# Matrix products that nobody reads, put into three pauses of TensorE in a two-layer attention and mixture-of-experts kernel

## What is computed

```python
x = x + _L0_attn_ref(_layernorm(x, axis=-1), L0_attn_Wq, L0_attn_Wk, L0_attn_Wv, L0_attn_Wo)   # causal, 16 heads of 8
x = x + _L0_ffn_ref(_layernorm(x, axis=-1), L0_ffn_router_w, L0_ffn_router_b, L0_ffn_w1, ...)  # 2 of 8 experts, 128 -> 512 -> 128
x = x + _L1_attn_ref(_layernorm(x, axis=-1), L1_attn_wq, L1_attn_wk, L1_attn_wv, L1_attn_wo)   # linear attention, no softmax
x = x + _L1_ffn_ref(_layernorm(x, axis=-1), L1_ffn_w_gate, L1_ffn_b_gate, L1_ffn_W1, ...)      # 1 of 8 experts
```

## Time and profile before

| | us |
|---|---|
| median of 3 runs | 666.56 (665.36 to 669.21) |
| profiled execution, its own time | 669.52 |
| span of its instructions | 667.4 |
| PE busy in the span | 532.7 (80%) |
| DVE busy | 449.2 (67%) |
| ACT busy | 354.0 (53%) |
| POOL busy | 342.5 (51%) |
| mean granted clock of PE | 0.893 |

### The profile page before, as it was taken

How to read it: one execution, slowest core, us unless ns; L and a number is a source line. 1 busy time by engine, 2 the same in 40 slices (tenths; PEclk the granted TensorE clock), 3 DMA queues, 4 the chain that set the end, 5 groups by cost and what they waited for, 6 DMA issues and landing times. The chain is left out here.

```text
span 667.4 us, 15359 instructions
## 1 busy us (share of the span) xinstructions
PE 532.7 (80%) x4916; PEld 439.3 (66%) x4931; DVE 449.2 (67%) x1287; ACT 354.0 (53%) x894; POOL 342.5 (51%) x459
## 2 busy tenths in 40 slices
PE   3189999999899998865989999999167561499996
PEld 2146666666666665643889989999155450498995
DVE  6476777878998797673777755553379877365662
ACT  2014457555655565443557656665347674265653
POOL 2003334434376536665746777776441547054555
PEclk9557999999999999987899999999567885699999
DMA  6563444445455445144423332221590125323330
GB/s 167 104 147 63 101 110 110 103 102 102 97 121 123 107 94 121 39 163 170 94 57 82 97 93 81 80 75 48 154 364 20 66 71 164 84 82 88 92 101 19
DMA packets 59525, 69.37 MB, mean 104 GB/s; under 512 B 9241, under 2 KB 50657, under 8 KB 57148
## 3 DMA queue, kind: packets, MB, share of 16 engines
q1 hardware_dynamic: 51168, 52.48, 31.6%
q0 software_dynamic: 7168, 14.77, 6.8%
q10 hardware_dynamic: 1116, 1.22, 0.9%
HBM read 45.31 MB, written 23.67 MB: 103 GB/s over the span
## 5 line engine op out<-in xcount | busy, mean ns | idle before, releaser
L616 DVE TENSOR_REDUCE mx<-max_ps 128x2 f32<-128x512 f32 (+1 forms) x192 | 128.4, 688 | 53.3 <-PE max_ps L277 51.4
L457 ACT ACTIVATE pT<-sc_ps 128x1536 f32<-128x1536 f32 x64 | 92.8, 1451 | 79.0 <-PE sc_ps L305 75.4
L1189 POOL DMA_INDIRECT expert_rows<-yt,go x72 | 78.7, 1093 | 28.6 <-issue 19.8
L1367 ACT ACTIVATE hT<-h_ps,wb 128x128 f32<-128x128 f32 x288 | 78.3, 386 | 20.2 <-PE h_ps L1414 20.2
L862 POOL TENSOR_TENSOR turn<-eps 128x1 f32<-128x1 f32 x64 | 12.6, 198 | 145.4 <-ACT pT L457 145.3
L58 POOL DMA_INDIRECT expert_queues<-rxr,rseats x64 | 65.7, 1026 | 26.8 <-issue 17.4
L1255 DVE COPY wb<-wpack 128x1156 f32 x72 | 53.6, 787 | 34.3 <-issue 26.9
L1414 PE MATMUL h_ps<-xT,wb 128*128 128x128 f32 x576 | 72.0, 279 | 0.5 <-ACT xT L1358 0.5
L274 PE MATMUL max_ps<-mask_qk,identb 128*128 128x256 bf16 (+1 forms) x177 | 57.5, 325 | 18.0 <-DMA wpack<-parts_scratch 13.9
L1532 POOL DMA_INDIRECT out_x<-yt,go x40 | 44.5, 1113 | 52.1 <-DVE go L1578 43.6
L1424 PE MATMUL y_ps<-wb,hT 128*128 128x128 f32 x576 | 70.0, 275 | 0.0
(11 more groups left out here) (307 smaller groups left out, 1113.1 us busy)
## 6 DMA issues: line engine op xcount, KB each, us to landing
wpack<-in_wpack SPq DMA_DIRECT2D x2, 4112.0 KB, 15.5
parts_scratch<-parts SPq DMA_DIRECT2D x16, 384.0 KB, 3.6
xt<-expert_queues SPq DMA_DIRECT2D x40, 129.0 KB, 2.1
xt<-expert_queues SPq DMA_DIRECT2D x72, 64.5 KB, 2.0
wpack<-parts_scratch SPq DMA_DIRECT2D x24, 192.0 KB
kst<-parts_scratch SPq DMA_DIRECT2D x24, 192.0 KB
qst<-parts_scratch SPq DMA_DIRECT2D x72, 64.0 KB
wpack<-parts_scratch SPq DMA_DIRECT2D x63, 64.0 KB
```

The source lines that it names most:

```text
L457: nc.scalar.activation(pT[u][:], sc_ps[:].rearrange("p a s -> p (a s)"), ACT.Exp, scale=float(DH) ** -0.5).then_inc(probs_ready, 1)
L616: nc.vector.reduce_max(mx[:, s, h0:h0 + n], max_ps[:, (k + 1) % 2, :].rearrange("p (h k) -> p h k", h=n), axis=AX.X).then_inc(unit_reduced, 1)
L1189: nc.gpsimd.indirect_dma_start(out=ys, out_offset=bass.IndirectOffsetOnAxis(ap=go[i % RING][:, s:s + 1].bitcast(mybir.dt.uint32), axis=0), ...
L1367: last = nc.scalar.activation(hT[i % 2][:, s, c, :], h_ps[i % 2][:, s, c * RT:(c + 1) * RT], ACT.Relu, bias=wb[i % 4][:, s, FF + c:FF + c ...
```

## The change

Three places get products whose result nobody reads. A function `warm(n)` inside PE's part of the attention multiplies the identity by the mask, 128x512 in bf16, into the bank `av_ps`; a function `warm(nc, t, bank, n)` does the same with two other constants, `before` (stationary) and `onesb` (moving, its 128 columns read four times). They have no semaphore of their own. Fifty stand in the prologue between `project_v` of sequence 0 and the first unit; eight in the tail behind `project_out`, ahead of the barrier; sixteen at the start of the first experts ahead of `transpose_in(0)`; ten at the start of the second experts ahead of `transpose_in(0, 0)`. The banks they write are overwritten by work with `start=True` before anything reads them. Nothing else is changed.

```diff
@@ causal_attention, PE
+            def warm(n):
+
+                for i in range(n):
+                    nc.tensor.matmul(av_ps[:], identb[:], t["mask_qk"][:].rearrange("p h k -> p (h k)"), start=True, stop=True)
@@ prologue
                 project_v(0, 0, 0, 2)
                 pe.wait_ge(mask_ready, 1)
+                warm(50)
                 for k in range(NU):
                     unit(0, 0, k)
@@ tail
                 project_out(b)
+                warm(8)
@@
+def warm(nc, t, bank, n):
+
+    for i in range(n):
+        nc.tensor.matmul(bank[:], t["before"][:], t["onesb"][:].unsqueeze(1).to_broadcast([P, 4, P]), start=True, stop=True)
@@ first_experts, PE
+            warm(nc, t, l_ps, 16)
             transpose_in(0)
@@ experts, PE
+            warm(nc, t, y_ps[1], 10)
             transpose_in(0, 0)
```

## The result

| | before | after |
|---|---|---|
| median of 17 runs each, us | 668.08 (665.36 to 671.71) | 671.33 (668.83 to 674.21) |
| profiled execution, us (span) | 669.52 (667.4) | 671.64 (669.7) |

The ratio is 1.0038, with a 95% interval of 1.0023 to 1.0053: the change costs 1.5 to 3.5 us (the medians alone differ by 3.25 us, a ratio of 1.0049, inside the interval). The forecast was +1.7 us. In absolute time the median lies 0.5 above the upper end of the range (670.8), because the median of before came out 1.5 higher in 17 runs than in the three on which the forecast stands.

A forecast was written before the change was run, and what follows sets the result against it. Opening: PE and DVE alternate, then PE bounds body 0; DVE bounds first barrier's release to 348. From 669.52, -0.5 + 2.2 + 0 + 0 gives 671.2; less 2.96 for the median, 668.3 us; range 663.8 to 670.8.

The forecast's parts named there:

- The barrier: First barrier: eight products at the low clock lengthen PE's DRAIN to about 4.7 us and delay everybody's release: +2.2 us.
- The opening: Prologue: fifty products raise the clock, which falls again after a pause; a first unit or two gain: -0.5 us.
- the units' possible gain: Opening's twelve units: at the high clock they would end at 41.6 instead of 43.1, 1.5 us earlier at most.
- The 4.7 for a surviving clock: Opening's upper limit with the clock high through body 0: 1.5 us from the units plus 3.2 from body 0.
- Case A: Opening: clock survives the pause and the units, or returns early in body 0: -3 to -4.7 us; chance 0.21.
- That the units and body 0 don't raise the clock any sooner once it is down: Opening: once low, the clock stays low as before, when it did so for 24 us with PE mostly busy.
- case C: Opening: the fifty don't raise the clock, body 0 is 7.6 us late, plus 2.2 at the barrier: 676.4; chance 0.04.
- The sixteen: Behind the first barrier: they fit the wait for rows, and DVE is the bound: 0, between -1 and +0.5 us.
- The ten: Second experts: they end at 571.1, PE idles 4.2 us, first tiles run at the low clock: 0 us.
- the signs that I named: Would show the forecast wrong: DVE waiting for PE between first barrier and choice, or the clock high at 575.
- -1.8: Second experts: value if the clock were high there, halving the 3.7 us up to 578.99.
- clock falling elsewhere by chance: Anywhere in the kernel: PE's clock falls elsewhere, 2 to 3 us to either side; chance 0.07.

The follow-up runs named there:

- forty_ahead: Kernel before plus only forty unread products ahead of the first barrier, on another chip: ratio 1.0123 (1.0066 to 1.0179) to the kernel before there.
- only_eight: Kernel before plus only the eight products ahead of the first barrier, on another chip: ratio 1.0052 (1.0017 to 1.0087) to the kernel before there.
- no_eight: Changed kernel without its eight products ahead of the barrier; fifty, sixteen and ten stay: ratio 1.0103 (1.0040 to 1.0166) to the kernel before on its chip.
- open_hold: Kernel before plus, in the opening only, sixty products, one behind each of twelve units and four ahead of the maxima's transposes: ratio 1.0006 (0.9974 to 1.0039).
- open_bridge: As open_hold, with thirteen more products behind the transposes of the maxima: ratio 1.0051 (1.0013 to 1.0088) to the kernel before, over all executions 0.9997.
- only_fifty: Kernel before plus only the fifty products in the opening, on another chip: ratio 0.9981 (0.9949 to 1.0013) to the kernel before there.
- only_sixteen: Kernel before plus only the sixteen products behind the first barrier, on another chip: ratio 1.0038 (1.0009 to 1.0066) to the kernel before there.
- only_ten: Kernel before plus only the ten products at the second experts, on another chip: ratio 0.9997 (0.9965 to 1.0029) to the kernel before there.
- after_again: The changed kernel, unchanged, rerun on a chip of the experiments: ratio 1.0064 (1.0016 to 1.0112) to the kernel before there, over all executions 1.0072.

## Why the prediction held, and where it did not

**The barrier** carried the sum, and in the trace of after it was right step by step: the eight at the low level, the DRAIN waiting for products that nobody reads, PE last instead of DVE, 34.5 us from release to choice, DVE with no wait for PE. I had +2.2 and the DRAIN at 4.7 us; it was +2.5 and 4.60. forty_ahead agrees that such a delay goes on to the end (9.1 for 8.3), and only_eight, with +1.2 to +6.4 us for a release 1.6 us later, doesn't speak against it. What I can't square with it is no_eight: without the eight the kernel should have come out near 1, and came out at 1.0103, with a delay in the attention and ahead of the choice that the missing products don't explain. That the eight are what the change costs is shown by after's trace and by forty_ahead, not by taking them out.

**The opening** was right in size (-0.5 expected, -0.4 at the first transposes, 0 at the second) and incomplete in its reason. I had the clock fall behind the pause, which it did, at 32.92. I put the units' possible gain at 1.5 us and let it pass to body 0. That step failed: the gain can be larger (2.3 us in open_hold, where twelve reductions take 7.91 us instead of the 8.7 of my sum), and a second transfer, the stack of sequence 1, arrives near 44.2 and lets hardly any of it through. The 4.7 for a surviving clock came out near 4.4 (open_bridge) by luck: the 1.5 of the units doesn't reach body 0, and body 0 alone gave 4.1 instead of 3.2. Case A asked for one pause to be survived, and there were two: the one of 2.27 us, and one of 2.99 us that opens ahead of body 0 once the units are faster. That the units and body 0 don't raise the clock any sooner once it is down did not hold in every trace: it came back for 3.41 us among the units of only_fifty, and for good at 47.55 in body 0 of only_sixteen. The Trainium skill, in the section that the prediction names, warns only of longer pauses than this first one of 2.27 us; with the units' thin work behind it the trace does not agree. Two figures of the prediction were wrong by its own numbers: case C needs about 14 of the fifty at the low level, not 18 (18.4 + 14 x 0.43 + 36 x 0.22 is 32.3), and the lower end of case A is 664.1, not 663.8 (668.8 - 4.7). Neither changes how the result is to be read.

**The sixteen** I had at 0, since DVE is the bound up to the choice. The trace of the first chip agrees. (The window that I wrote as 5.73 - 4.4 is 318.02 - 313.6 = 4.4; the value used was right.) What I did not see is that a PE that is further ahead also pauses longer: 3.45 us instead of 2.4 at the choice, and in this execution the clock fell. Whatever of the 0.37 us behind the choice is due to it lies inside the +0.5 that I had as the upper bound. The term rests on DVE waiting for nobody, and on the chips of the experiments it does not hold: DVE waits there for PE, PE for ACT.

**The ten** I had at 0, with the clock low from 566.8 to 578.99. One of the signs that I named came out otherwise: I had written that I would be wrong if the clock was high at 575, and it was, for a stretch in which PE had no work. That step failed: the ten raised the clock after all, too late for themselves and too early for the rows. The value 0 held all the same, as far as can be told: the +0.9 of this execution lies inside what kernels without the ten differ by. -1.8, which I had given for a high clock, assumed that it would last to the first tile; only_ten and after_again show a gain of that size (1.2 to 1.7) where the rows come right behind them.

The bridge, 1.9 us shorter in after's profiled execution, is not touched by the change. PE's mean granted clock is 0.71 there against 0.68:

```profile
470.70:567.50 96.80, 46.09 (x271) 38.35 (x271) 72.91 (x346) 57.75 (x171) 46.61 (x65) 0.71 0.45 142
```

That is the "clock falling elsewhere by chance" of the prediction. It was named and sized (2 to 3 us); whether it was chance wasn't tested. In this pair of traces it offsets what the first and the second experts take more (0.37 and 1.34 us).

## What to carry to other kernels

Products that nobody reads are work for every wait that counts work: here the DRAIN at the end of a block waited for them and all engines with it. Ahead of a barrier they cost their time as soon as the engine's slack (0.95 us here) is used up. A raised clock is worth something only if no pause lies between the filling and the first work for which PE is the bound, and if no transfer or engine behind it takes the gain: look for the next transfer before pricing the clock. A filling of fixed length fits one arrival time; where the arrival moves between 4.4 and 8.5 us from run to run, ten products are too few in one place and twenty-six too many in another. And before a difference of 1 us at one place is put down to a change, look at how much that place varies between kernels that leave it alone.

## What the runs showed of the hardware

The clock can rise when the work that raised it is over: at 572.23 the last of the ten ended, and 3.41 us at the high level passed with PE idle. It can fall just ahead of the work behind a pause, 0.25 us at 350.36 and 0.68 at 575.64, or just behind its begin, 0.65 us at 32.92. So the price of a pause is paid by what follows it. Ahead of the choice of experts the same shows in fourteen traces: the clock fell in or behind the pause in the three with 2.99, 3.02 and 3.45 us (only_fifty, only_ten, after), and not in the eleven with 1.3 to 2.4 us.

In the opening, where only units follow, the clock fell with less: 2.27 us of idle time in after, and in after_again 1.64 us (it fell at 32.49, 1.46 us after work had begun again). In open_hold and open_bridge, with no pause ahead of the units and one more product of 128 rows behind each, it stayed high to the units' end. Which of the two held it wasn't tested.

The same program takes 668 us on one chip and 733 to 740 on others. The difference lies mostly in the same places (the attention's bodies 10, 11, 14 and 15 of 16, which take 1 to 12 us more, the first experts behind the choice, 27 to 31 us more, and the bridge, 10 to 16 us more); in the attention and the first experts in pauses that the profile puts down to nothing it shows. A gain of 4.4 us made before the first of them was not to be found behind it in the one trace that has it.
